# DLRM forward on one core: inner pairs stored round the circle of fields, 85 rows stacked three deep, bt 3's gram moved by GpSimd

## The reference

```python
sparse_embed = emb_tables[field_idx[None, :], x_sparse]        # 512 x 26 x 64
z = sparse_embed.reshape(B, N_FIELDS * K)                      # 1664 columns
gram = jnp.einsum('bik,bjk->bij', sparse_embed, sparse_embed)
iu, ju = jnp.triu_indices(N_FIELDS, k=1)
inner = gram[:, iu, ju]                                        # 325 columns
dnn_in = jnp.concatenate([x_dense, z, inner], axis=-1)         # 2002 columns
h = jax.nn.relu(dnn_in @ w1 + b1)
out = jax.nn.sigmoid(h @ w2 + b2)
```

## Time and profile before

| | |
|---|---|
| median of 3 runs | 209.91 us (209.57 to 210.88) |
| profiled execution, device time | 209.74 us |
| its span, first to last instruction | 207.4 us |
| TensorE busy | 198.8 us (96%) |
| VectorE, ScalarE, GpSimd busy | 145.0, 131.2, 128.8 us |
| DMA | 39.00 MB, mean 188 GB/s |
| granted TensorE clock | 1.00 throughout |

### The profile page before, as it was taken

How to read it: one execution, slowest core, us unless ns; L and a number is a source line. 1 busy time by engine, 2 the same in 40 slices (tenths; PEclk the granted TensorE clock), 3 DMA queues, 4 the chain that set the end, 5 groups by cost and what they waited for, 6 DMA issues and landing times.

```text
span 207.4 us, 3878 instructions
## 1 busy us (share of the span) xinstructions
PE 198.8 (96%) x1340; PEld 161.4 (78%) x1340; DVE 145.0 (70%) x340; ACT 131.2 (63%) x263; POOL 128.8 (62%) x210
## 2 busy tenths in 40 slices
PE   8899988999999999999999899999999999999993
PEld 8766867788788888877887688888888887788882
DVE  3665927886939868788579899294687599573573
ACT  2755516686978859986377735595899985642201
POOL 4888889888988889629888888898950000000000
PEclk9999999999999999999999999999999999999999
DMA  5389999897585814326977657858597359123100
GB/s 149 100 258 291 280 342 342 286 304 267 136 308 128 308 35 97 67 50 180 304 268 217 180 165 213 327 152 302 172 268 287 99 136 331 40 47 57 30 0 0
DMA packets 15388, 39.00 MB, mean 188 GB/s; under 512 B 3881, under 2 KB 5281, under 8 KB 15369
## 3 DMA queue, kind: packets, MB, share of 16 engines
q1 hardware_dynamic: 11688, 35.27, 51.6%
q0 software_dynamic: 3328, 3.41, 8.3%
q10 hardware_dynamic: 353, 0.08, 0.2%
HBM read 37.71 MB, written 0.69 MB: 185 GB/s over the span
## 4 chain that ended last, share of the span: by engine, by line
PE 78%; POOL 9%; DVE 5%; DMA 4%; issue 3%; ACT 1%; DVEq 0%; ACTq 0%
PE slot L1081 23%; PE slot L1084 22%; PE slot L1087 22%; POOL E L824 8%; PE slot L1041 4%; DMA E<-emb,row_idx 3%; PE slot L1071 2%; DVE G L979 2%; PE slot L1072 2%; PE slot L1073 2%; DVE w_lo L931 1%; DMA x_idx<-idx 1%; POOL pace L834 1%; DVE slot L1005 1%; ACT w_hi L849 0%
## 5 line engine op out<-in xcount | busy, mean ns | idle before, releaser
L824 POOL DMA_INDIRECT E<-emb,row_idx x104 | 111.1, 1069 | 24.1 <-issue 16.9
L931 DVE TENSOR_TENSOR w_lo<-w_raw,w_hi 128x500 fp32r<-128x500 f32 (+6 forms) x128 | 79.9, 669 | 15.0 <-ACT w_hi L849 14.7
L849 ACT CAST w_hi<-w_raw 128x1000 fp32r<-128x1000 f32 (+6 forms) x64 | 64.9, 1029 | 26.4 <-DMA w_raw<-w 20.2
L1081 PE MATMUL slot<-w_hi,x_hi 128*128 128x500 f32 (+5 forms) x236 | 74.6, 397 | 3.8 <-ACT x_hi L875 2.6
L1084 PE MATMUL slot<-w_lo,x_hi 128*128 128x500 f32 (+5 forms) x236 | 72.9, 390 | 0.0
L1087 PE MATMUL slot<-w_hi,x_lo 128*128 128x500 f32 (+5 forms) x236 | 72.7, 389 | 0.0
L1081 PEld LDWEIGHTS slot<-w_hi,x_hi 128*128 128x128 f32 (+2 forms) x236 | 43.4, 189 | 14.7 <-ACT x_hi L875 4.1
L1084 PEld LDWEIGHTS slot<-w_lo,x_hi 128*128 128x128 f32 (+2 forms) x236 | 44.5, 188 | 9.4 <-DVE w_lo L931 0.3
L1087 PEld LDWEIGHTS slot<-w_hi,x_lo 128*128 128x128 f32 (+2 forms) x236 | 44.5, 189 | 9.2
L880 ACT COPY ET<-T 32x128 f32<-32x128 f32 (+4 forms) x94 | 34.1, 363 | 2.2
L948 DVE STREAM_TRANSPOSE T<-E 128x256 f32<-128x256 f32 x24 | 10.6, 441 | 17.2 <-DMA E<-emb,row_idx 17.1
(11 more groups left out here) (39 smaller groups left out, 82.8 us busy)
## 6 DMA issues: line engine op xcount, KB each, us to landing
w_raw<-w SPq DMA_DIRECT2D x32, 501.0 KB, 4.8
...
E<-emb,row_idx POOLq DMA_INDIRECT x104, 3.5
...
```

The lines of the kernel that those rows point to most:

```text
L824: nc.gpsimd.indirect_dma_start(out=E[:, k % ER, j, :], out_offset=None, in_=emb_rows, in_offset=bass.IndirectOffsetOnAxis(ap=row_idx[:, at ...
L849: nc.scalar.copy(w_parts(m)[0], w_source(m)).then_inc(w_hi_ready, 1)
L931: nc.vector.tensor_tensor(lo[:, cols], w_source(m)[:, cols], hi[:, cols].bitcast(F32), ALU.subtract)\
L1081: nc.tensor.matmul(acc[q], xh, hi[:, cols[q]], start=first, stop=False)
```

## The change

**Layout.** The fields are seen as a circle: a pair is (i, i + d) with d from 1 to 13 (modulo 26). All pairs now go by way of DRAM: `around` stores the whole gram and the first 13 columns once more behind it, `skewed` fetches six rectangles of it (`PAIRS_AT`). No pair goes straight from G to x_in.

**Tiles.** There are four inner tiles. FULL_0 and FULL_1 (t15, t16) are products of three passes as before. TERMS_A and TERMS_B (t13, t14) share 85 rows (`BOTH`: 78 pairs and 7 dense columns): tile A's x is their x_hi, its weights their w_lo; tile B's x is their x_lo, its weights their w_hi. The remaining rows of the two tiles hold the three terms of other rows, so that each of the two is one pass (2 matmuls). A cell's inner part is 1 + 1 + 3 + 3 = 8 passes where it was 3 x 3 = 9. Pieces: 68 loads where there were 64, 16 of them inner (12 before). A TERMS_B piece has no w_lo; its x_lo needs the x_hi of both tiles.

**Who moves.** SP stores and fetches bt 0 to 2; GpSimd does it for bt 3, behind its gathers. A fetch is six DMAs, a store two (before: two fetches, two stores and three direct DMAs). The dense columns are loaded by SP rather than ScalarE, `x_idx`, `ones` and others lie in G until it is needed.

**Order.** `make_todo` mixes the inner steps otherwise, puts the last gram rounds later by one to two steps, and B1's last z tiles (t10, t11) ahead of B2's t4 and t5; the planner's costs of a move are new.

```diff
-CROSS = [(0, 9), (9, 12), (12, 13)]
-IT = len(CROSS)
+IT = 4
+TERMS_A, TERMS_B, FULL_0, FULL_1 = range(ZT, NT)
+BOTH = 6 * HALF + 7
+PAIRS_AT = [(TERMS_A, 0, 20, 26, HALF), (TERMS_A, BOTH + 3, 20, 23, HALF), (TERMS_B, BOTH + 4, 23, 26, HALF),
+            (FULL_0, 0, 0, 7, HALF), (FULL_0, 7 * HALF, 7, 10, HALF - 1), (FULL_1, 7, 10, 20, HALF - 1)]
...
-    todo += q5[:1] + mixed(gram({1}), q5[1:] + inner_0[:1], per=2)
+    todo += q5[:1] + mixed(gram({1}), q5[1:] + inner_0[:2], per=2)
...
-        todo += b_group("B2", 0, GROUP_ORDER[n]) if n < 4 else []
-    rest = [s for g in GROUP_ORDER[4:] for s in b_group("B2", 0, g)]
-    todo += mixed(rest[:7], gram({2, 3}), every=2) + rest[7:]
+        todo += b_group("B2", 0, GROUP_ORDER[n]) if n < 3 else []
+    rest = [s for g in GROUP_ORDER[3:] for s in b_group("B2", 0, g)]
+    todo += rest[:1] + mixed(rest[1:9], gram({2, 3}), every=2) + rest[9:]
...
+STORE_AT, FETCH_AT = 0.3, 3.6
+MOVE_LAND = (4.4, 5.2, 6.8, 7.6)
...
+        def around(bt):
+
+            rows, to = Q * (bt % 2), gram_dram[bt, 0:FIELDS * AROUND].rearrange("(i j) b -> i j b", i=FIELDS)
+            return [(to[:, 0:FIELDS, :], G[rows:rows + FIELDS, :, :]),
+                    (to[HALF:FIELDS, FIELDS:AROUND, :], G[rows + HALF:rows + FIELDS, 0:HALF, :])]
+
+        def skewed(bt):
+
+            src = gram_dram[bt].rearrange("(i s) b -> s i b", i=FIELDS)
+            return [(t - ZT, x_in[at:at + far * (b - a), bt, t - ZT, :], src[1:far + 1, a:b])
+                    for t, at, a, b, far in PAIRS_AT]
...
                 if op[0] == "store":
-                    for m, (a, b) in enumerate(CROSS):
-                        sp.dma_start(x_in[CROSS_AT[m]:CROSS_AT[m] + HALF * (b - a), bt, m, :],
-                                     G[rows + a:rows + b, HALF:FIELDS, :]).then_inc(x_in_landed[bt][m], 16)
+                    for to, src in around(bt):
+                        sp.dma_start(to, src).then_inc(g_stored[bt], 16)
                 if op[0] == "fetch":
                     bt = op[1]
                     sp.wait_ge(g_stored[bt], 32)
+                    for m, to, src in skewed(bt):
+                        sp.dma_start(to, src).then_inc(x_in_landed[bt][m], 16)
...
+            pool.wait_ge(g_copied_act, evac_count("act", rounds_of(POOLED)))
+            pool.wait_ge(g_copied_dve, evac_count("dve", rounds_of(POOLED)))
+            for to, src in around(POOLED):
+                pool.dma_start(to, src).then_inc(g_stored[POOLED], 16)
+            pool.wait_ge(g_stored[POOLED], 32)
+            for m, to, src in skewed(POOLED):
+                pool.dma_start(to, src).then_inc(x_in_landed[POOLED][m], 16)
...
+                    if t in (TERMS_A, TERMS_B):
+                        if t == TERMS_A:
+                            pe.wait_ge(x_hi_ready, x_hi_count(*key_of(step)))
+                        else:
+                            pe.wait_ge(x_split, x_lo_count(*key_of(step)))
+                            pe.wait_ge(w_hi_ready, w_hi_count(RANK[n]))
+                        for q in (0, 1):
+                            if t == TERMS_A:
+                                pe.wait_ge(w_split, w_split_count(RANK[n], q))
+                            last = nc.tensor.matmul(acc[q], xh, hi[:, cols[q]], start=first, stop=end)
```

205 lines of the change are left out of this document (117 added, 88 removed).

## The result

The changed kernel takes **219.32 us** (median of 4 runs, 217.16 to 220.26), the one before, run beside it, 209.76: ratio 1.0415, 95% interval 1.0362 to 1.0467. Medians are over all executions and ratios over the fast ones alone (some executions of every kernel are slower), so a ratio needn't be the quotient of two medians. The prediction had the sign and the places of the loss right (the middle, where bt 1's inner tiles wait, and with it the start of phase B) and the size wrong: 213.3 us, range to 216.2; most of what it missed lies at the end, for which it counted 0.3 us. The profiled execution took 220.26 us with a span of 218.3; before 209.74 and 207.4. The passes went as counted (1,324 matmuls for 1,340), so what has to be found is 10.9 us of span, and on top the 3.64 that were saved.

What follows compares the result with a forecast made beforehand. TensorE was taken as the bound, busy 198.8 of 207.4 us. From 209.74 us, + 5.1 (later phase B) - 1.82 (passes of bt 2 and 3) + 0.3 (end) = + 3.6 gave 213.3 us, range 209.3 to 216.2.

Steps and rivals of the forecast that it cites:

- The passes, -3.64 us: TensorE, inner part: one pass of nine goes in 8 cells, 8 x 0.455 = 3.64 us, half in phase A, half at the end.
- The price of the store: SP's stores, middle and end: each lands 2.7 us after its issue; behind weights, bt 1's lands 1.3 us after the eighth piece.
- Six fetch issues, 5.1 us: SP, middle: bt 0's fetch of six DMAs takes 4.9 to 5.7 us, 5.1 taken, from 89.4 to 94.5 us.
- Pieces at 1.6 us each, the eighth cast at 101.6: Phase A's last inner weight pieces: sixth lands at 98.4, two more at 1.6 us each; eighth there at 101.6, cast at 102.7.
- bt 1's first inner x_hi at 106.7: Middle: TensorE gets it at 105.5 or 106.8 us, 106.7 taken, instead of 100.0, behind bt 1's store and a weight cast.
- From there 8.0 us to phase B: Middle, after bt 1's first inner x_hi: 1.1 us, three passes of 0.455, four products of 1.365; phase B at 114.7.
- Early phase B, no difference: Start of phase B: TensorE's wait for an x_hi behind a weight cast stays about as before, 0 to 3 us.
- The end, +0.3: After the last gram round: bt 2 hardly late, bt 3 by GpSimd up to 1.7 us late; 0.3 us taken.
- The sum: Whole kernel: + 5.1 at phase B's start, - 1.82 for passes, + 0.3 at the end, = + 3.6 on 209.74 us.
- Rival: the gathers take the place: Middle stalls stay small; TensorE waits for bt 3's last gathered x_hi at 158.84 us; 209.3 us, no change; chance 0.25.
- Rival: GpSimd slow: End: GpSimd's eight direct DMAs for bt 3 take 4.3 us more, 2 to 3 us net on top; 216 us; chance 0.10.
- The range: Total time: 209.3 to 216.2 us, taking in the gathers' case and most of the slow end; mechanism alone + 1.9 to + 7.8.

Runs made afterwards that it cites:

- floor run: Changed kernel with 169 KB stores, fetches reading only those, pieces 31 and 32 before bt 0's fetch, last weight piece before bt 2's store: 209.92 us, ratio 0.9941.

## Why the prediction was wrong, step by step

- **The passes, -3.64 us:** as counted.
- **The price of the store: the step that failed.** "bt 0's store lands 2.7 us after" was read where a store was 0.17 MB and was put on one of 0.43 MB. It measured 3.8 for bt 0, 6.9 for bt 1, 4.4 for bt 2 and 8.0 for bt 3; with 169 KB it was 1.6 for bt 0. The prediction knew that the store is now 0.43 MB and used it only for bt 1, as time behind the weights (1.3 us). What the store does to the weight pieces queued beside it was put at nothing: at 171 to 198 GB/s it is over 2 us of nearly full DMA engines, four times (an estimate), and the kernel's last piece landed in 9.3 us. With stores of 169 KB and all else alike phase B began at 113.83 (114.7 predicted), the wait in the tail was 0.21 us, and the loss was gone. The trace of before had a sign of it, though mixed with the direct moves that ran beside the store, 121 GB/s at a DMA share of 0.81:

```profile
88.00:89.00 1.00, 1.00 (x27) 0.87 (x19) 0.58 (x2) 0.66 (x3) 0.00 (x0) 1.00 0.81 121
```

- **Six fetch issues, 5.1 us:** 5.75, just above the 4.9 to 5.7 read from the rows. With the store's 0.6 us SP was free at 95.80 for 94.5.
- **Pieces at 1.6 us each, the eighth cast at 101.6:** cast at 103.67.
- **bt 1's first inner x_hi at 106.7, from 105.5 or 106.8:** 108.99 (cast at 108.64). The two values differed by what the order on the ring is worth; the measured one lies 2.2 us above both.
- **From there 8.0 us to phase B:** 10.1. The clock was taken as 1.00, but behind the predicted waits it fell to 0.50; where it didn't, the stretch took 7.7 and 8.0 us. A stall had to be priced with its clock.
- **Early phase B, no difference:** the wait of 1.07 us before went, as TensorE came 9.4 us later; together with smaller ones a gain of 1.9 us (119.06 to 185.57 is 66.5 us for 71.2 before, two products of 1.37 fewer).
- **The end, +0.3:** +5.2, the largest single miss. From the last gram round to the end 32.7 us, 26.6 before, two products more and four passes fewer: 0.9 of the 6.1 explained, the rest is the wait of 3.61 and about 1.6 of half clock (12 matmuls in 4.35 us). bt 2 "hardly late" rested again on the 2.7 us, and the piece "in between" was seen, but not that its cast stands ahead of every inner x_hi while two stores run beside its load.
- **The sum:** 9.4 - 1.9 - 1.8 + 5.2 = 10.9, the span that was to be found. Against the predicted + 3.6 that is 2.3 more up to bt 1's x_hi, 2.1 of clock, 1.9 less in phase B and 4.9 more at the end.
- **Rival: the gathers take the place.** Not reached: the floor run began phase B at 111.86, close to the 111.5 given, and shows no wait for x_hi near 158. Neither supported nor refuted.
- **Rival: GpSimd slow.** Refuted for its issues: 0.56 us each, ratio 1.0512 without it. Its store landed late, in 8.0 us, and in 4.6 with stores of 169 KB: that is the price of the stores again.
- **The range** ended at 216.2 although the mechanism's own bounds, + 7.8, reach 217.5; the measured time is above both. Every bound was of one kind, DMA times taken from lighter traffic. The bounds' values (4.7 for the fetch, 1.4 and 2.1 for a piece, 4.3 to land) are also not those that its own rows gave (4.9, 1.3 and 1.95, 3.9).
